# First experts of a two-layer decoder: who requests the first pages, who adds the shared rows, and one product block moved ahead of the counts

## The reference

```python
scores = softmax(xt @ Wg.T)            # 16 experts, 4 groups, top 2 groups, top 4 experts
combine = zeros((T, E)).at[arange(T)[:, None], topi].add(weights)
h = silu(einsum('td,eid->eti', xt, W1)) * einsum('td,eid->eti', xt, W3)   # 176 wide
y = einsum('etd,te->td', einsum('eti,edi->etd', h, W2), combine)
z = silu(xt @ Ws1.T) * (xt @ Ws3.T) @ Ws2.T                               # shared experts
return y + z
```

## Time and profile before

| | us |
|---|---|
| median of 3 runs | 1177.14 |
| lowest, highest | 1175.23, 1184.77 |
| profiled execution | 1178.34 |
| its span, first to last instruction | 1176.5 |
| PE busy | 1067.4 (91%) |
| DVE busy | 505.0 (43%) |
| ACT busy | 498.5 (42%) |
| POOL busy | 441.9 (38%) |

### The profile page before, as it was taken

The page is one execution under the profiler, slowest core; times in us unless marked ns, Lnnn a source line. Parts: engine busy times, 40 slices in busy tenths (PEclk is TensorE's granted clock), DMA queues, the critical chain, the costliest instruction groups (busy, mean ns, idle before and its releaser), DMA issues. The chain is left out here.

```text
span 1176.5 us, 28787 instructions
## 1 busy us (share of the span) xinstructions
PE 1067.4 (91%) x10240; PEld 819.7 (70%) x10241; DVE 505.0 (43%) x1373; ACT 498.5 (42%) x1278; POOL 441.9 (38%) x563
## 2 busy tenths in 40 slices
PE   7889998899888769999988999998689999999998
PEld 4466666666445547777556777777479899899897
DVE  2365655655582113333635566657363700000413
ACT  2444545444432223333335556675344333333333
POOL 2032131311138871778826656522513000200534
PEclk9999999999999989999999999998799999999999
DMA  6189369031193344565454111100167555555673
GB/s 204 42 303 364 118 212 354 10 101 55 63 301 116 126 138 125 149 193 157 121 222 160 44 41 38 28 20 3 68 216 234 178 169 179 186 166 175 203 240 105
DMA packets 117325, 174.27 MB, mean 148 GB/s; under 512 B 17216, under 2 KB 94896, under 8 KB 115760
## 3 DMA queue, kind: packets, MB, share of 16 engines
q1 hardware_dynamic: 93440, 134.63, 35.2%
q0 software_dynamic: 9696, 26.75, 6.9%
q10 hardware_dynamic: 14080, 11.36, 3.0%
HBM read 104.15 MB, written 67.24 MB: 146 GB/s over the span
## 5 line engine op out<-in xcount | busy, mean ns | idle before, releaser
L3258 PE MATMUL bank<-w,m_HT 128*128 x624 | 141.0, 379 | 0.0
L3093 ACT ACTIVATE m_HT<-bank,m_b 128x128 f32<-128x128 f32 x312 | 88.7, 368 | 89.6 <-PE bank L3244 71.9
L3258 PEld LDWEIGHTS bank<-w,m_HT 128*128 128x128 f32 x624 | 115.7, 190 | 14.1
L1911 PE MATMUL bank<-m_W,m_XGT 128*128 x256 | 90.5, 477 | 8.1 <-ACT m_XGT L1743 8.0
L1495 POOL DMA_INDIRECT GA<-ys,r_pos x64 | 64.6, 1010 | 50.0 <-DVE m_US L1830 29.7
L3057 POOL DMA_INDIRECT m_GA<-ys,r_pos x32 | 31.4, 982 | 129.5 <-SPq L3013 120.4
L3244 PE MATMUL bank<-m_XGT,m_w1a 128*128 128x128 f32 x640 | 77.2, 279 | 2.6 <-issue 1.8
L3244 PEld LDWEIGHTS bank<-m_XGT,m_w1a 128*128 128x128 f32 x640 | 75.0, 195 | 3.4 <-issue 2.3
L1743 ACT ACTIVATE m_XGT<-bank 128x256 f32<-128x256 f32 x72 | 27.6, 383 | 113.7 <-DVE m_US L1830 74.5
L1680 POOL DMA_INDIRECT xs<-X,r_pos x64 | 63.8, 997 | 29.7 <-issue 15.2
L1822 DVE TENSOR_TENSOR m_H<-bank,m_SG 128x176 f32<-128x176 f32 x72 | 24.5, 341 | 111.8 <-ACT m_SG L1747 93.6
(11 more groups left out here) (518 smaller groups left out, 2349.1 us busy)
## 6 DMA issues: line engine op xcount, KB each, us to landing
m_w1a<-in_m_w SPq DMA_DIRECT2D x20, 1024.0 KB
m_w<-in_m_w SPq DMA_DIRECT2D x19, 1024.0 KB
xs<-zeros SPq DMA_DIRECT2D x1, 9216.0 KB, 32.9
ys<-zeros SPq DMA_DIRECT2D x1, 9216.0 KB, 32.2
ys<-m_US ACTq DMA_DIRECT2D x72, 128.0 KB
m_GS<-xs SPq DMA_DIRECT2D x65, 128.0 KB
w<-in_m_w SPq DMA_DIRECT2D x8, 1024.0 KB, 9.4
xs<-zeros SPq DMA_DIRECT2D x1, 7296.0 KB, 26.1
```

Source lines behind the costliest of these rows:

```text
L1911: last = nc.tensor.matmul(BU[b % 2][:, 0:IW], XGT[:, b % 2, m * P:(m + 1) * P], W13[:, m, bass.ds(e, 1), :], start=m == 0, stop=m == KC - 1)
L3093: last = nc.scalar.activation(HT[:, b % 2, at, :], BU[i][:, c * P:(c + 1) * P], ACT.Gelu, bias=b1[:, b % WB, at:at + 1])
L3258: last = nc.tensor.matmul(BY[b % 2][:, 0:DIM], HT[:, b % 2, c, :], w2[:, bass.ds(e, 1), c, :], start=c == 0, stop=c == CH - 1)
```

## The change

POOL does 7 gates instead of 6, and DVE 5; the gates in `fills` move up by one with it, and none is left before the maximum in `ready_on_dve`. POOL no longer adds Z: DVE adds one whole tile, t = j - 8, at the end of steps 8 to 23, and `add_rows` of tile t waits for it. SP requests pages 0 to 7; page 0 waits for 11 gates and page 2 for 12. ACT makes its two copies of Z before it waits for the page table. On PE the gate side of chunk 6 stands ahead of the counts.

```diff
-    POOL_GATES = 2 * SC
-    FIRST, CHECKED = 7, 32
+    POOL_GATES = 2 * SC + 1
+    FIRST, CHECKED, ADDS = 7, 32, 8
@@ sync
-                load(FIRST, FIRST % 4, FIRST)
+                for j in range(FIRST + 1):
+                    if j in (0, 2):
+                        sp.wait_ge(sh_h, SC * GROUPS - 1 + j // 2)
+                    load(j, j % 4, j)
@@ gpsimd
-                        if t and k % 2:
-                            add_shared(t - 1, k // 2)
                 landed(TILES - 1)
-                for half in range(2):
-                    add_shared(TILES - 1, half)
-                pool.wait_ge(z_added, 2 * TILES)
...
                     pool.wait_ge(gathered[t % 2], 16 * TOP0 * (t // 2 + 1))
+                    pool.wait_ge(z_added, t + 1)
@@ scalar
                 act.wait_ge(sh_h, SC * GROUPS)
-                act.wait_ge(r.placed, 2)
-                for j in range(4):
-                    load(j, j)
                 shared_rows(PAIRS - 4)
                 shared_rows(PAIRS - 3)
+                act.wait_ge(r.placed, 2)
                 rows(0, 0)
-                load(4, 0)
                 rows(1, 1)
-                load(5, 1)
...
-                load(6, 2)
@@ vector
                 r.ready_on_dve(nc, dve, fx.ident[:], BU[0], BU[1], 2, gated,
-                               ((POOL_GATES + 3,), (POOL_GATES + 4,)))
-                gated(POOL_GATES + 5)
+                               ((), (POOL_GATES + 3,)))
+                gated(POOL_GATES + 4)
...
-                    if n == 0:
-                        dve.wait_ge(z_added, 2 * TILES)
...
+                def step_and_add(j, b, ahead):
+                    step(j, b, ahead)
+                    t = j - ADDS
+                    x = fx.X[:, bass.ds(t, 1), :]
+                    dve.wait_ge(in_place, t + 1)
+                    nc.vector.tensor_tensor(x, x, Z[:, bass.ds(t, 1), :], ALU.add).then_inc(z_added, 1)
...
+                with dve.Fori(0, ADDS // 4) as i:
+                    for b in range(4):
+                        step(i * 4 + b, b, None)
+                dve.wait_ge(z_used, PAIRS)
+                with dve.Fori(ADDS // 4, (ADDS + TILES) // 4) as i:
+                    for b in range(4):
+                        step_and_add(i * 4 + b, b, None)
@@ tensor
                 shared_up(1)
+                shared_up(2, (0,), (0,))
                 r.on_pe(nc, pe, fx.before, fx.ones, BH[0], BH[1])
                 shared_down(0)
-                shared_up(2)
+                shared_up(2, (0,), (1,))
+                shared_up(2, (1, 2))
```

More of the change, by code:

```diff
@@ L1671, in landed @@
                     pool.sem_inc(in_place, 1)
[L1673 to L1676, removed]
                 for t in range(TILES):
@@ L1853, in keep_down @@
                     down_step[n] = r.steps.k
+                def step_and_add(j, b, ahead):
[4 more added lines that the diff above has]
+                    nc.vector.tensor_tensor(x, x, Z[:, bass.ds(t, 1), :], ALU.add).then_inc(z_added, 1)
                 product(0, 0)
                 product(1, 1)
-                tile_pipeline(dve, step, NT, ((44, lambda: fx.l1.moments_on_dve(nc, dve, fx.X, r.steps)),), peel=16)
+                with dve.Fori(0, ADDS // 4) as i:
[5 more added lines that the diff above has]
+                        step_and_add(i * 4 + b, b, None)
+                tile_pipeline(dve, step, NT, ((44, lambda: fx.l1.moments_on_dve(nc, dve, fx.X, r.steps)),),
+                              done=ADDS + TILES, peel=16)
             @block.tensor
@@ L1861, in _, with shared_up @@
                 pe.sem_inc(t_full, 4)
-                def shared_up(g, parts=range(SC)):
+                def shared_up(g, parts=range(SC), sides=range(2)):
                     for c in parts:
                         n = SC * g + c
-                        for i in range(2):
+                        for i in sides:
                             if n > SC:
```

## The result

The changed kernel takes 1208.26 us (1207.76 to 1210.45, three runs) against 1177.14: ratio 1.0239, 95% interval [1.0209, 1.0269]. It is 31 us slower; 1167.6 was forecast.

What follows compares the result with a forecast made beforehand. Pages were taken to be slow because PE's results reach other engines late while POOL densely issues indirect DMAs. An 11.0 us earlier release, less lost pages, gave 9.5 us: 1178.34 to 1168.8, less 1.2 for the median, 1167.6; range 1151 to 1181.

Steps and rivals of the forecast that it cites:

- Adds leave POOL: POOL's scatter: without 29 half adds at 0.38 us each, the last scatter starts 11.0 us earlier, near 425.6.
- Adds on DVE at cost 0: Steps 8 to 23: 16 adds of 0.42 us, 6.8 us of DVE work, cost 0, at worst 6.8.
- Product block and gates: Before the counts: block and gate 6 earlier, but table copied at 358.0 to 358.4; shared stage gets nothing back.
- Loads on SP: First pages: SP requests them, ACT's 8.26 us idle goes, first output at 388.8, 4.7 us earlier; bounds -1.1 to 6.
- The sum: Whole kernel: 11.0 us from the earlier release less pages lost, gain 8.3 to 10.5, taken as 9.5: 1167.6 us.
- Outputs copied before the release: Pages during the scatter: 7.8 intervals now; after, in 38.8 us, 6.7 at 5.81 us or 7.6 at 5.1.
- outputs over 7 us apart: Sign of being wrong: output copies over 7 us apart while POOL scatters.
- the full starving: Scatter: no page done at 427.6, 19.5 us lost against 11.0 won, time 1186; half of the 0.14.
- the starving rival: Scatter: dense DMAs with gaps of only 0.30 us starve the pages; slower, 1172 to 1192 us; chance 0.14.
- the burst at 826: Indirect DMAs at 826.48: PE goes on, a group of matmuls each 0.73 us; six scatters around 825 let results through.
- the main case: Whole kernel: 9.5 us gained, pages still 5 to 6 us apart during the scatter, 1164 to 1171 us; chance 0.48.

Runs made afterwards that it cites:

- adds_only: Kernel before with only the adds of Z moved from POOL to DVE: 1131.56 us against 1130.43, ratio 1.0001.
- the fillers: Whole change plus unused POOL additions of constants between scatters: ratios 1.0067, 0.9929 and 0.9831 for three main spacings where the kernel before takes about 1180 us.
- after_again: The whole changed kernel unaltered, run on another chip: 1124.28 us against 1132.49 for the kernel before, ratio 0.9937.
- A: The part of the change that moves the adds to DVE; alone on the kernel before: 1131.56 us, ratio 1.0001.
- L: The part that moves the first eight page loads to SP; alone on the kernel before: 1130.05 us, ratio 1.0006.
- P: The part with the product block ahead of the counts and POOL's seventh gate; alone on the kernel before: 1135.03 us, ratio 1.0031.
- adds_loads: Kernel before with adds on DVE and loads on SP, without the product block and seventh gate: 1205.03 us, ratio 1.0211.
- adds_pe: Kernel before with adds on DVE and the block ahead of the counts, loads left on ACT: 1209.60 us, ratio 1.0258.
- bare_and_early: Kernel before with the product block, seventh gate and loads on SP, adds left on POOL: 1130.69 us, ratio 0.9986.
- gap_early: Changed kernel with an unused 128x128 POOL addition after every scatter of the second to seventh tile only: 1128.36 us, ratio 0.9987.
- gap_each_full: Changed kernel with an unused 128x128 POOL addition of constants after every scatter: 1161.63 us, ratio 0.9831.
- gap_each_16: Changed kernel with an unused 128x16 POOL addition after every scatter: 1126.74 us, ratio 0.9980; repeated on another chip 1193.90 us, ratio 1.0115.

## Why the prediction was wrong

**Adds leave POOL**: right. 29 x 0.38 = 11.0 us off the scatter were forecast; from first to last start it lasts 80.9 us against 92.2, 11.3 less, and it starts 2 us later on the first chip.

**Adds on DVE at cost 0**: right. They take 0.42 us each in both kinds of trace. adds_only can't be told from the kernel before, and the fillers remove the loss with the adds in place. By the Trainium skill's rule (SBUF — State Buffer, SBUF: two separate sides) an add that meets a POOL operation reading SBUF might have been held up. Of the 16 in after_again the median is near the shortest, and the two longest are those beside POOL's first scalings of gathered rows:

```profile
L1840 DVE TENSOR_TENSOR X<-X,m_Z x16: 415/416/631, 409.0 to 446.4; - x16
444.00 0.62 DVE L1840 TENSOR_TENSOR X<-X,m_Z  x1
444.56 0.49 POOL L1511 TENSOR_SCALAR GA<-GA,r_wt 128x256 f32<-128x256 f32 x1
446.27 0.48 POOL L1511 TENSOR_SCALAR GA<-GA,r_wt 128x256 f32<-128x256 f32 x1
446.40 0.63 DVE L1840 TENSOR_TENSOR X<-X,m_Z  x1
```

Each is 0.2 us longer than the rest. The trace so agrees that such a pair costs something; as the bars overlap, it does not show a whole instruction's wait.

**Product block and gates**: right on chips Q, where the table is copied at 358.37 (forecast 358.0 to 358.4). On the first chip it came at 360.18, and there the scatter too starts 1.8 us later (346.56 against 344.75), so the steps between are the same. Alone the part costs 0.3% on a chip Q.

**Loads on SP**: right on chips Q: ACT's idle 8.26 us before the pair of Z copies is gone, first output at 388.06 (forecast 388.8).

**The sum**: this step failed. "Outputs copied before the release" took 5.81 us a page, or 5.1, as what a page takes beside a scatter, and treated it as a property of the kernel. It was a point on a steep curve: at a mean of 1.47 us from scatter to scatter a page takes 5.8, at an even 1.59 it takes 2.5, and at 1.28 not one passes. The prediction's own sign of being wrong, outputs over 7 us apart, is what came, and its range ended at 1181, below the 1186 at which it priced the full starving. The text had half of the cause ("what PE finishes reaches the other engines late while POOL issues"), and the starving rival had the right sign; that SP's page requests stall as well, it did not see. The rival got 0.14, and its price, 1186, was 22 us short for two reasons. It applied the stall from the first page on (388.8), while the shared experts' products cross the same way (the first such wait, 7.3 us, ends at 379.95, before there are pages), so that the first output itself moved by 55.6 us. And it let the stall end with the last scatter, while ACT saw its rows only 8 us after it. With the measured 449.1 in it, the rival's sum reads 449.1 + 17 x 2.5 = 491.6 for the first gather against 461.6, which is 30 of the 31 us; nothing before the run gave the 449.1.

What spoke for it stood in the earlier trace rows: 7.04 us without a result beside eight back-to-back gathers. Against it I set the burst at 826, where results pass every 0.73 us, and that row described another spacing and other work. The answer from which the earlier trace rows is taken has a second line, which the prediction did not use:

```profile
SPq L1626 <- remote: 11.0, 4, 3.6
```

**On chips Q** the forecast of the main case, 9.5 us gained, stands against 8.2 measured. That is luck, and its working is not confirmed by it: pages there pass at 2.5 us all along, so no page was lost or won in the stall, and the parts do not add up to it (A 0, L 0, P +0.3%, L and P -0.1%, all three -0.6%). Which meeting of A with the others makes the 8 us was to be read from adds_loads and adds_pe; both ran on a chip S, so it stays open. The first gather does not settle it: it stands at 436.0 in adds_only, 442.8 in bare_and_early, 432.4 in after_again, and only the last is faster.

Open as well: what differs between the two kinds of chip (or between two states of a chip), and by which path a transfer issued by POOL holds up a completion of PE and a request of SP or ACT. One rival was not tested: every time here is of an execution whose span the profiler recorded, and the distances of SP's requests in the stall (14.0, 14.0 and 14.7 us) are multiples of the 0.70 us that its register moves take there. So the recording itself may take part in the stall, and whether an execution without it has the stall is not known. gap_early was not seen on a chip S, gap_each_full not on a chip Q, so that no version is shown to beat both kernels on both kinds. On chips S gap_each_full beats both (1161.6 against 1179.7 and 1208.3); on chips Q the change as it is does (1124.3), and gap_each_16 lies 0.2% under the kernel before.

## What to carry to other kernels

Useful work that sits between an engine's transfer issues may be the pause that lets everyone else's results through; before moving it away, price what happens at the new spacing, from the densest burst in the trace and not from the mean of the present one. A stall seen at one spacing is no constant, and it can begin before the stage of interest does. Waits marked "remote" and page requests that go out far apart with nothing to wait for are the signs to look for, and a small change should be timed on more than one chip before it is kept or dropped.

## What the runs showed of the hardware

- Chips differ in this by more than most edits are worth: the same kernel before takes 1130 to 1132 us on two chips and 1177 to 1180 on the others (whether chip or state is open), and the change is -0.6% on the one kind and +2.1 to +2.6% (its variants with one part missing) or +2.4% (whole) on the other.
- On the slower kind PE's completions are seen late by ACT and DVE while POOL issues indirect DMAs: by 57.8 us at a mean of 1.28 us from one to the next (after), while in gap_each_full, at 1.59 us, no wait is put down to "remote" as long as the scatter lasts. The mean steps of the two, 1.28 and 1.62 us, differ by 0.34 us, and their times by 47 us.
- In the same stall the engine that requests page loads slows down as well: SP's first four requests stand 14.0 to 14.7 us apart (378.5 to 421.2) and its register moves take 0.70 us, against 1.7 to 2.1 us and 0.03 us in after_again; in adds_pe it is ACT that has two requests 14.0 us apart.
- The lateness outlives the scatter: ACT saw work that PE had done before 379 only at 436.66, 8 us after the last scatter ended.
- PE's granted clock in the starved stage was 0.54 (391.6 to 439.2), near the lower of its two levels (1.2 of 2.4 GHz), against 1.00 in the same stretch of gap_each_full; PE's work there is 7.2 us of 47.6. So the low clock goes with PE's idle time here; with the fillers PE is busy throughout (47.6 us of 47.6) and the clock is 1.00.
